# Last block of layer 2: order of the uncertainty branch, Tanh for Sigmoid, re-placed value products; one product of the up step ahead of the levels

## The chip, the cores and the metric

The kernel runs on one core of a Trainium2 chip. The metric is the time of one execution in microseconds on the device. A core has TensorE (PE), VectorE (DVE), ScalarE (ACT), GpSimd (POOL) and SyncE (SP, which issues DMAs). Each engine runs its own list of instructions in order; they wait for each other by semaphores. All matrix products are in fp32; each is two instructions on PE.

## The reference

A chain of four layers on 2048 tokens (64 sequences of 32) of width 512; each is a conditioning map and a feed-forward map, added to x. The change touches three places.

Layer 1's feed-forward is a gated product with a hidden width of 1376, its three weights quantised to 16 levels first:

```
h = silu(x @ w1.T) * (x @ w2.T);  x = x + h @ w3.T        (w1, w2, w3 after quantise and dequantise)
```

Layer 2's feed-forward (its input h is the output of layer 2's conditioning):

```
query = h @ Wq.T;  rq = query @ Wr.T;  rk = aux_keys @ Wr.T
scores = rq . rk / sqrt(48) + log_rel;  top 8 of 128 slots
w = softmax(query . key / 8 + log_rel) over the 8
aux_out = (w @ aux_values) @ Wvd.T @ Wvu.T
norm_var = log1p(var(h)) / (mean(log1p(var(h))) + 1e-6)
learned = gelu(h @ Wu1.T + bu1) @ Wu2.T + bu2
u = clip(norm_var * 0.5 + sigmoid(learned) * 2.5, 0, 5)
gate = sigmoid(gate_w1 * clip((u - 0.5) / 1.5, 0, 1) + gate_bias);  gate = 0 where gate < 0.05
result = h + gate * aux_out
```

Layer 3 averages x over each sequence under a mask, convolves the 32 (padded) means per feature, takes a sigmoid as a gate over x, and applies a linear map with a mixture of eight low-rank terms; the mixture weights of each second token come from a softmax, a top-2 threshold and a sigmoid.

## The kernel before

Tokens are handled in four blocks of 512 (TB = 4); x lies transposed in SBUF, features on partitions in four chunks (DC = 4). A product over one chunk and one block is 128x512; its two instructions take 0.43 us each. PSUM has eight banks of 128x512, `ps[:, bank, :]`.

*Up step of layer 1.* The 44 steps of the list `UPS` (L231) are pairs of token block and hidden chunk c (11 chunks, the last has 96 rows). `up(n)` on PE (L1040) computes both halves into banks n % 2 and 2 + n % 2. The steps with c = 10 put gate and up half into one bank (L1050 on). ACT (L804 to L825) runs, for each n, first its share of the *levels* (`parts_of(K_UP, n, ...)`, L747: a saturated comparison of a weight unit with one of 15 quantisation bounds), then the SiLU of step n, then a copy of a turned weight unit (`evac_quant`). DVE (L1608 to L1612) runs, for each n, its share of levels (L1513, L1516: add the step height; between units it prepares the next one, L1487 to L1494) and then, for c = 10 only, `hidden(n)` (up to L1605), the product of SiLU and up half; for the others POOL does it. PE's step n waits for the product or the copy of step n - 2, whose banks it overwrites. Step 33 is (block 3, c = 10).

*Layer 2, block tb.* On PE in this order: the conditioning's products, q (L1230 to L1234; two halves on 64 columns each), the wide uncertainty product into bank 4 (`p_gup`), 16 turns of Y to natural order for the variances (L1237), the scores (`p_sc`, banks 6 and 7), the learned product (bank 5, `p_lr`). In the last block, PE fills its waits with `slices`, narrow products for layer 3. ACT copies q, applies Gelu (L872), copies the learned column (L874), in the last block Ln of the variances (L878) and Sigmoid (L880), and then Exp of the selected scores (L885). DVE takes statistics (L1786), selects the top 8 per token (L1798 to L1803), and after the last block computes the uncertainty (L1805 to L1816), lets ACT take the gate (L888, Sigmoid), and scales the probabilities (L1824). PE turns them (L1266), ACT copies them (L893), `slices_aux` completes the narrow products, from which DVE computes the sequence gates (L1836 to L1848); `aux(n)` (16 products of the turned probabilities with the values) go to the banks `BANKS_AUX`, and DVE adds each to X (`add_aux`, L1830). `spread_gates` broadcasts the gates to banks 0 to 3, `base(n)` are layer 3's 16 products, `ranks` and `lift` its low-rank part.

ACT loads a function table (`ACT_TABLE_LOAD`) when the next function is not in the table it holds.

Of the kernel before, what the change touches and what calls it, by code (L numbers as in the profile page):

```python
# [16 lines left out]
P = 128  # L17
# [76 lines left out]
def build(nc, A, out):  # L94
    ctx = ExitStack()
    with ctx:
# [114 lines left out]
        gsc = sb("gsc", [P, 3])  # L211
# [22 lines left out]
        in_u = [Up[:, i % DC, i // DC * TW:(i // DC + 1) * TW] for i in range((TB - 1) * DC)]  # L234
        PLAIN = [i for i, (tb, c) in enumerate(UPS) if c < NH - 1]
# [129 lines left out]
        BANKS_AUX = 3 * [6, 7, 4, 5] + 2 * [4, 5]  # L365
# [351 lines left out]
        def _(act):  # L717
# [139 lines left out]
            for tb in range(TB):  # L857
# [12 lines left out]
                nc.scalar.activation(qT[0:BOT, TW // 2:], ps[BOT:, 1, 0:TW // 2], ACT.Copy).then_inc(s["a_q"], 1)  # L870
                act.wait_ge(s["p_gup"], tb + 1)
                nc.scalar.activation(gu, ps[:, 4, :], ACT.Gelu_apprx_tanh, bias=bu1[:, 0:1]).then_inc(s["a_gu"], 1)  # L872
                act.wait_ge(s["p_lr"], tb + 1)
                nc.scalar.activation(lrn[:, tb * NT:(tb + 1) * NT], ps[:, 5, 0:NT], ACT.Copy).then_inc(s["a_lr"], 1)  # L874
                if tb == TB - 1:

                    act.wait_ge(s["d_st"], TT + 1)
                    nc.scalar.activation(lv[:, :], var[:, :, 1], ACT.Ln, bias=1.0, accum_out=lvs[:, 0:1]).then_inc(s["a_lv"], 1)  # L878
                    act.wait_ge(s["a_lr"], TB)
                    nc.scalar.activation(gq[:, 0, :], lrn[:, :], ACT.Sigmoid, bias=gsc[:, 2:3]).then_inc(s["a_sg"], 1)  # L880
# [7 lines left out]
            nc.scalar.activation(gq[:, 2, :], gq[:, 1, :], ACT.Sigmoid, scale=gsc[:, 0:1], bias=gsc[:, 1:2]  # L888
# [30 lines left out]
        def _(pe):  # L919
# [250 lines left out]
            for tb in range(TB):  # L1170
# [54 lines left out]
                for c in range(DC):  # L1225
                    last = mm(ps[:, 4, :], l2u[:, c, :], Y[:, c, tok(tb)], c == 0, c == DC - 1)
                last.then_inc(s["p_gup"], 1)
# [16 lines left out]
                last.then_inc(s["p_sc"], 1)  # L1244
                pe.wait_ge(s["a_gu"], tb + 1)
# [23 lines left out]
            slices(1, range(0, 2))  # L1269
            pe.wait_ge(s["a_lv"], 1)  # L1270
            pe.wait_ge(s["a_lr"], TB)
            mm(ps[:, 5, 8:9], ones[:, :], lvs[:, 0:1], True, True).then_inc(s["p_lv"], 1)
            slices(1, range(2, DC))
            for tb in range(3):
                turn_probs(tb)
            slices_aux(0)
            turn_probs(3)
            slices_aux(1)

            def aux(n):  # L1280

                tb, oc = n // DC, n % DC
                if n >= 12:
                    pe.wait_ge(s["d_x3"], n - 1)
                elif n >= 4:
                    pe.wait_ge(s["d_x3"], n - 3)
                mm(ps[:, BANKS_AUX[n], :], v2[:, oc * P:(oc + 1) * P], PT[:, tok(tb)], True, True).then_inc(s["p_aux"], 1)

            def base(n):

                tb, oc = n // DC, n % DC
                if n < 2:
                    pe.wait_ge(s["a_g"], TB)
                    pe.wait_ge(s["d_x3"], DC)
                elif n < 4:
                    pe.wait_ge(s["d_x3"], 8 + BANKS_AUX.index(BANKS3[n]) + 1)
                elif n < 6:
                    pe.wait_ge(s["d_x3"], TB * DC - 5 + n)
# [7 lines left out]
            def spread_gates(pair):  # L1306
                pe.wait_ge(s["d_gex"], pair + 1)
                if pair == 0:
                    pe.wait_ge(s["a_zt"], TB)
                    pe.wait_ge(s["d_yd"], 2)  # L1310
                for j in range(2):
# [17 lines left out]
            for n in range(6):  # L1329
# [13 lines left out]
            base(2)  # L1343
            base(3)
# [5 lines left out]
            aux(12)  # L1350
            aux(13)
            for half in range(2):
                ranks(half)
            aux(14)
            aux(15)
# [10 lines left out]
        def _(dve):  # L1366
# [251 lines left out]
            ts(lbias[:, :, :], lbias[:, :, :], 5.0, None, ALU.mult, ALU.bypass)  # L1618
            for q in range(2):
# [187 lines left out]
            dve.wait_ge(s["p_lv"], 1)  # L1807
            dve.wait_ge(s["a_sg"], 1)
            ts(lvs[:, 1:2], ps[:, 5, 8:9], 1.0 / TOK, 1e-6, ALU.mult, ALU.add)
            link(V.reciprocal(lvs[:, 1:2], lvs[:, 1:2]))  # L1810
            ts(gq[:, 1, :], lv[:, :], lvs[:, 1:2], None, ALU.mult, ALU.bypass)
            ts(gq[:, 1, :], gq[:, 1, :], 0.5, None, ALU.mult, ALU.bypass)
            stt(gq[:, 1, :], gq[:, 0, :], 2.5, gq[:, 1, :], ALU.mult, ALU.add)
            ts(gq[:, 1, :], gq[:, 1, :], 0.0, 5.0, ALU.max, ALU.min)
            ts(gq[:, 1, :], gq[:, 1, :], 0.5, 1.0 / 1.5, ALU.subtract, ALU.mult)
            V.tensor_scalar(gq[:, 1, :], gq[:, 1, :], 0.0, 1.0, ALU.max, ALU.min).then_inc(s["d_un"], 1)  # L1816
# [128 lines left out]
```

## Time and profile before

| | us |
|---|---|
| median of three runs | 909.38 (909.37 to 910.17) |
| the profiled execution's own time | 909.91 |
| its span | 908.1 |
| PE busy | 856.7 (94%) |
| DVE busy | 615.3 (68%) |
| ACT busy | 411.9 (45%) |
| POOL busy | 153.2 (17%) |

The span runs from the first to the last recorded instruction; all positions are microseconds from its start. The weight loads of PE (PEld) overlap its products.

### The profile page before, as it was taken

Reading aid. Unit: us, or ns where it says so; the run is one execution under the profiler, and the core shown is the slowest. Engines: PE = TensorE matmul, PEld = TensorE weight load, DVE = VectorE, ACT = ScalarE, POOL = GpSimd, SP = SyncE. Lnnn points to the kernel's source line nnn. Section 1 sums busy time; section 2 is a strip of 40 time slices with the busy share of each in tenths; the row PEclk is TensorE's granted clock in tenths of the full one; section 3 lists DMA queues with packets and bytes.
Section 4 is the critical chain, followed back from the end, with each engine's and each line's share of the span. In section 5 each row is a group of like instructions: output and inputs, shape, how many; then the busy total and the mean of one; then the engine's idle time right before and its main releaser. Section 6 shows DMA issues by size and latency. Waiting matters only on the chain.

```text
span 908.1 us, 10585 instructions
## 1 busy us (share of the span) xinstructions
PE 856.7 (94%) x3265; PEld 458.4 (50%) x3266; DVE 615.3 (68%) x956; ACT 411.9 (45%) x531; POOL 153.2 (17%) x174
## 2 busy tenths in 40 slices
PE   0599999999999999999989999999999999979998
PEld 0496448998444444444444444444445555443442
DVE  7799987887888888899998744253452354256624
ACT  5124647886787777877878520000012132252100
POOL 5200008800121212221102110002401011010000
PEclk9999999999999999999999999999999999989999
DMA  6696138550000000100000110013010000002012
GB/s 184 239 340 229 58 116 282 199 209 31 23 23 24 5 13 32 33 17 16 32 1 0 41 49 1 0 58 128 15 51 1 1 0 1 1 1 46 35 58 93
DMA packets 34729, 60.98 MB, mean 67 GB/s; under 512 B 6040, under 2 KB 8424, under 8 KB 34040
## 3 DMA queue, kind: packets, MB, share of 16 engines
q1 hardware_dynamic: 33896, 60.26, 19.4%
q0 software_dynamic: 704, 0.10, 0.3%
q8 instruction: 26, 0.43, 0.2%
q14 instruction: 23, 0.19, 0.1%
q10 hardware_dynamic: 80, 0.01, 0.0%
HBM read 50.84 MB, written 8.47 MB: 65 GB/s over the span
## 4 chain that ended last, share of the span: by engine, by line
PE 86%; DVE 7%; issue 3%; POOL 2%; ACT 2%; DMA 0%; SPq 0%; POOLq 0%; ACTq 0%; DVEq 0%
PE ps L921 84%; DVE acc L1516 2%; DVE T L1516 1%; PE ps L979 1%; PE ps L1237 1%; DVE W2T L1377 1%; DMA T<-kpad 0%; PE ps L1266 0%; DVE raw L1494 0%; DVE amax L1487 0%; DVE Yp L1890 0%; POOL lan_i L648 0%; ACT Yp L862 0%; PE ps L1199 0%; DVE Yp L1529 0%
## 5 line engine op out<-in xcount | busy, mean ns | idle before, releaser
L747 ACT ACTIVATE above<-raw,cst 128x1024 bf16<-128x1024 f32 (+2 forms) x225 | 272.0, 1233 | 121.3 <-DVE acc L1516 43.7
L1516 DVE SCALAR_TENSOR_TENSOR acc<-above,acc 128x1024 f32<-128x1024 bf16 (+2 forms) x112 | 150.5, 1344 | 28.7 <-ACT above L747 24.7
L921 PE MATMUL ps<-Yp,W3T 128*128 (+1 forms) x740 | 159.5, 370 | 3.2 <-DVE Yp L1529 1.6
L921 PE MATMUL ps<-Up,W2T 128*128 128x512 f32 (+1 forms) x404 | 160.6, 593 | 0.0
L921 PE MATMUL ps<-Up,W1T 128*128 128x512 f32 x344 | 155.5, 594 | 2.8 <-DVE Up L1605 2.6
L1516 DVE SCALAR_TENSOR_TENSOR T<-above,T 128x1024 f32<-128x1024 bf16 (+1 forms) x84 | 118.1, 1405 | 22.7 <-ACT above L747 19.6
L921 PEld LDWEIGHTS ps<-Yp,W3T 128*128 128x128 f32 x740 | 102.3, 191 | 55.5 <-issue 52.9
L921 PEld LDWEIGHTS ps<-Up,W2T 128*128 128x128 f32 (+1 forms) x404 | 66.5, 177 | 85.9 <-issue 85.6
L921 PEld LDWEIGHTS ps<-Up,W1T 128*128 128x128 f32 x344 | 64.2, 190 | 82.1 <-issue 75.8
L921 PE MATMUL ps<-X,W3T 128*128 128x512 f32 (+1 forms) x176 | 77.8, 596 | 0.3 <-DVE X L1830 0.3
L921 PE MATMUL ps<-X,W2T 128*128 128x512 f32 x140 | 61.3, 594 | 0.0
L921 PEld LDWEIGHTS ps<-X,W3T 128*128 128x128 f32 (+1 forms) x176 | 32.9, 190 | 43.4 <-issue 41.8
L1636 DVE TENSOR_TENSOR Yp<-Yp,ps 128x512 f32<-128x512 f32 x14 | 9.4, 685 | 59.8 <-PE ps L921 59.8
L921 PE MATMUL ps<-Up,W3T 128*128 128x256 f32 (+3 forms) x196 | 45.5, 388 | 0.0
L921 PEld LDWEIGHTS ps<-X,W2T 128*128 128x128 f32 x140 | 26.3, 190 | 31.9 <-issue 31.9
L688 POOL TENSOR_TENSOR Yp<-Yp 128x512 f32<-128x512 f32 x13 | 19.9, 1534 | 120.3 <-ACT Yp L819 120.3
L921 PE MATMUL ps<-W1T,W2T 128*128 128x512 f32 (+1 forms) x144 | 36.0, 436 | 3.6 <-DVE W2T L1459 3.6
L708 POOL TENSOR_TENSOR X<-X,Yp 128x2048 f32<-128x2048 f32 x4 | 18.1, 4520 | 124.5 <-ACT Yp L862 124.5
L921 PEld LDWEIGHTS ps<-Up,W3T 128*128 128x128 f32 (+1 forms) x196 | 30.9, 191 | 13.4 <-issue 12.5
L688 POOL TENSOR_TENSOR X<-X,Yp 128x512 f32<-128x512 f32 x15 | 21.7, 1447 | 78.3 <-ACT X L819 78.3
L684 POOL COPY Yp<-X x44 | 34.1, 825 | 2.3 <-issue 2.3
L818 ACT ACTIVATE Yp<-ps 128x512 f32<-128x512 f32 x40 | 23.3, 582 | 20.4 <-PE ps L921 20.3
(336 smaller groups left out, 882.7 us busy)
## 6 DMA issues: line engine op xcount, KB each, us to landing
W3T<-in_wa SPq DMA_DIRECT2D x8, 1024.0 KB, 5.8
raw<-in_w SPq DMA_DIRECT2D x20, 256.0 KB, 3.0
W3T<-kpad SPq DMA_DIRECT2D x9, 512.0 KB, 6.9
Up<-in_xconv SPq DMA_DIRECT2D x4, 1024.0 KB, 12.1
X<-in_xT SPq DMA_DIRECT2D x4, 1024.0 KB, 8.7
W1T<-in_wa SPq DMA_DIRECT2D x4, 1024.0 KB, 6.5
xkeep<-X SPq DMA_DIRECT2D x4, 1024.0 KB, 4.7
X<-xkeep SPq DMA_DIRECT2D x4, 1024.0 KB, 9.0
```

The source lines that it names most:

```text
L684: pool.tensor_copy(Y[:, :, bass.ds(t * (4 * S) + i * S, S)], X[:, :, bass.ds(b * S, S)]).then_inc(s["g_xs"], 1)
L688: nc.gpsimd.tensor_tensor(slots[UPS[n]], slots[UPS[n]], sg[n % 2], ALU.mult).then_inc(s["g_h"], 1)
L708: nc.gpsimd.tensor_tensor(X[:, :, tok(tb)], X[:, :, tok(tb)], Y[:, :, tok(tb)], ALU.add).then_inc(s["g_xc"], 1)
L747: nc.scalar.activation(above[0:h, m % 2, 0:w], raw[0:h, u % 2, 0:w], ACT.Relu, scale=STEEP, bias=cst[0:h, C_BND + i:C_BND + i + 1]).then_i ...
L818: nc.scalar.activation(sg[n % 2][0:h, :], ps[0:h, n % 2, :], ACT.Silu).then_inc(s["a_silu"], 1)
L921: return nc.tensor.matmul(o, l, r, start=start, stop=stop, **kw)
L979: last = nc.tensor.transpose(dst, src, ident[0:h, 0:h])
L1237: last = nc.tensor.transpose(ps[:, BANKS_ST[t], c * P:(c + 1) * P], Y[:, c, tile(tb, t)], ident)
L1377: link(V.tensor_tensor(o, a, b, op))
L1516: V.scalar_tensor_tensor(out=ac, in0=src, scalar=float(STEPS[i]), in1=ac, op0=ALU.min, op1=ALU.add).then_inc(s["m_used"], 1)
L1636: V.tensor_tensor(o, a, b, op).then_inc(s["d_mix"], 1)
```

## The change

- On ACT, the SiLU of step 33 stands ahead of that step's levels; on DVE the product of step 33 does.
- In the last block of layer 2, PE's wide product (now `rise`) stands behind the scores; the mean product of the logarithms (now in bank 2) and one chunk of `slices(1)` follow it, then the learned product, then the other three chunks.
- On ACT, Ln stands ahead of Gelu. The learned column is not copied in the last block: sigmoid is computed as (1 + tanh(x/2)) / 2, the first twelve columns from the copies, the last four from PSUM. The gate, too, is a Tanh. Four small DVE instructions prepare the halved scales once.
- DVE computes the uncertainty with one clip to [0.5, 2.0] in place of two; the divisor 2 goes into the softmax's denominators.
- The value products use banks 2 and 3 too; aux(0) stands between the last turn and the second `slices_aux`, aux(6) and (7) between the spreads, aux(12) and (13) ahead of base(3), and aux(14) and (15) ahead of `ranks`. Additions 14 and 15 stand ahead of those of zq. The waits for banks follow the list.

```diff
-        BANKS_AUX = 3 * [6, 7, 4, 5] + 2 * [4, 5]
+        BANKS_AUX = [6, 7, 4, 5, 2, 3, 6, 7, 4, 5, 6, 7, 4, 5, 4, 5]
+        AUX_LAST = {b: n + 1 for n, b in enumerate(BANKS_AUX)}
...
             for n, (tb, c) in enumerate(UPS):
                 h = HCH[c]
-                for k in parts_of(K_UP, n, AD_LAST):
-                    level(k)
+                if n != LAST_REST:
+                    for k in parts_of(K_UP, n, AD_LAST):
+                        level(k)
                 act.wait_ge(s["p_gu"], n + 1)
...
+                if n == LAST_REST:
+                    for k in parts_of(K_UP, n, AD_LAST):
+                        level(k)
                 for u in turns_up(n):
                     evac_quant(u)
...
+                if tb == TB - 1:
+                    act.wait_ge(s["d_st"], TT + 1)
+                    nc.scalar.activation(lv[:, :], var[:, :, 1], ACT.Ln, bias=1.0, accum_out=lvs[:, 0:1]).then_inc(s["a_lv"], 1)
                 act.wait_ge(s["p_gup"], tb + 1)
                 nc.scalar.activation(gu, ps[:, 4, :], ACT.Gelu_apprx_tanh, bias=bu1[:, 0:1]).then_inc(s["a_gu"], 1)
...
+                else:
+                    act.wait_ge(s["a_lr"], TB - 1)
+                    nc.scalar.activation(gq[:, 0, 0:TT - NT], lrn[:, 0:TT - NT], ACT.Tanh, scale=0.5, bias=gsc[:, 3:4])
+                    act.wait_ge(s["p_lr"], TB)
+                    nc.scalar.activation(gq[:, 0, TT - NT:], ps[:, 5, 0:NT], ACT.Tanh, scale=0.5, bias=gsc[:, 3:4]
+                                         ).then_inc(s["a_sg"], 1)
...
-            nc.scalar.activation(gq[:, 2, :], gq[:, 1, :], ACT.Sigmoid, scale=gsc[:, 0:1], bias=gsc[:, 1:2]
+            nc.scalar.activation(gq[:, 2, :], gq[:, 1, :], ACT.Tanh, scale=gsc[:, 4:5], bias=gsc[:, 5:6]
...
+                if tb == TB - 1:
+                    rise()
+                    pe.wait_ge(s["a_lv"], 1)
+                    mm(ps[:, 2, 0:1], ones[:, :], lvs[:, 0:1], True, True).then_inc(s["p_lv"], 1)
+                    slices(1, range(0, 1))
...
+            for tb in range(3):
+                turn_probs(tb)
+            slices_aux(0)
+            turn_probs(3)
+            aux(0)
+            slices_aux(1)
+            for n in range(1, 6):
                 aux(n)
             spread_gates(0)
+            aux(6)
+            aux(7)
             spread_gates(1)
-            for n in range(6, 12):
+            for n in range(8, 12):
                 aux(n)
...
             for n in range(TB * NH):
+                if n == LAST_REST:
+                    hidden(n)
                 for k in parts_of(K_UP, n, AD_LAST):
                     level(k)
-                if n not in PLAIN:
+                if n not in PLAIN and n != LAST_REST:
                     hidden(n)
...
+            ts(lvs[:, 1:2], ps[:, 2, 0:1], 2.0 / TOK, 2e-6, ALU.mult, ALU.add)
+            link(V.reciprocal(lvs[:, 1:2], lvs[:, 1:2]))
+            ts(gq[:, 1, :], lv[:, :], lvs[:, 1:2], 1.25, ALU.mult, ALU.add)
             dve.wait_ge(s["a_sg"], 1)
...
+            stt(gq[:, 1, :], gq[:, 0, :], 1.25, gq[:, 1, :], ALU.mult, ALU.add)
+            V.tensor_scalar(gq[:, 1, :], gq[:, 1, :], 0.5, 2.0, ALU.max, ALU.min).then_inc(s["d_un"], 1)
             dve.wait_ge(s["a_pr"], TT)
-            link(V.reciprocal(gq[:, 3, :], den[:, :]))
+            ts(gq[:, 3, :], den[:, :], 2.0, None, ALU.mult, ALU.bypass)
+            link(V.reciprocal(gq[:, 3, :], gq[:, 3, :]))
             dve.wait_ge(s["a_gt"], 1)
...
+            stt(gq[:, 3, :], gq[:, 2, :], 1.0, gq[:, 3, :], ALU.add, ALU.mult)
+            stt(gq[:, 4, :], gq[:, 2, :], 2 * 0.05 - 1.0, gq[:, 3, :], ALU.is_ge, ALU.mult)
```

## Rows read from the trace of the kernel before

**Rows 1.** The page's first part: busy us, share of the span, instructions of each engine
```profile
PE 856.7 (94%) x3265; PEld 458.4 (50%) x3266; DVE 615.3 (68%) x956; ACT 411.9 (45%) x531; POOL 153.2 (17%) x174
```

**Rows 2.** Waits of PE, 200 to 909: who waited for whom, us, times, longest
```profile
PE ps L1266 <- DVE W1T L1824: 5.6, 1, 5.6
PE ps L921 <- DVE Up L1605: 2.6, 1, 2.6
```

**Rows 3.** Timeline 446 to 476: start us, us, engine, instruction, [idle before <- releaser]
```profile
456.12 1.36 PE L979 MATMUL ps<-cst,acc 128*128 128x128 f32 x11
461.46 4.94 DVE L1516 SCALAR_TENSOR_TENSOR T<-above,T 128x1408 f32<-128x1408 bf16 x3
463.18 1.47 ACT L747 ACTIVATE above<-raw,cst 128x1408 bf16<-128x1408 f32 x1 [5.62 <-DVE T L1516]
464.68 0.59 ACT L823 ACTIVATE Yp<-ps 64x512 f32<-64x512 f32 x1
...
466.44 0.69 DVE L1605 TENSOR_TENSOR Up<-Yp,ps 64x512 f32<-64x512 f32 x1
...
467.18 3.70 PE L921 MATMUL ps<-Up,W1T 128*128 128x512 f32 x8 [2.64 <-DVE Up L1605]
...
469.92 0.61 ACT L819 ACTIVATE Up<-ps 128x512 f32<-128x512 f32 x1
```

**Rows 4.** Timeline, the end of the up step
```profile
515.75 1.63 DVE L1522 TENSOR_TENSOR acc<-acc,amax 128x1408 f32<-128x1408 f32 x1
...
523.42 1.36 PE L979 MATMUL ps<-cst,acc 128*128 128x128 f32 x11
```

**Rows 5.** Windows: length, busy of PE PEld DVE ACT POOL, PE clock, DMA share, GB/s
```profile
466.00:467.00 1.00, 0.00 (x0) 0.00 (x0) 0.96 (x2) 1.00 (x4) 0.00 (x0) 1.00 0.00 0
...
668.00:669.00 1.00, 0.72 (x16) 0.55 (x20) 0.54 (x7) 0.73 (x2) 0.00 (x0) 0.50 1.00 389
...
811.00:811.50 0.50, 0.00 (x0) 0.00 (x0) 0.00 (x0) 0.50 (x1) 0.00 (x0) 0.72 0.00 0
...
818.00:818.50 0.50, 0.50 (x8) 0.05 (x1) 0.00 (x0) 0.00 (x0) 0.00 (x0) 0.95 0.00 0
```

**Rows 6.** Timeline 780 to 806: q with the wide product, Gelu, the learned product
```profile
794.30 5.58 PE L921 MATMUL ps<-Yp,raw 128*64 128x256 f32 x24
...
799.91 0.69 ACT L872 ACTIVATE Up<-ps,bu 128x512 f32<-128x512 f32 x1 [1.55 <-PE ps L921]
...
803.33 0.95 PE L921 MATMUL ps<-wu,Up 128*128 128x1 f32 x8
```

**Rows 7.** Timeline 805 to 815: row maximum, gate, first scaling, first turns
```profile
807.92 0.69 DVE L1803 TENSOR_REDUCE Up<-Up 128x4 f32<-128x512 f32 x1
...
812.86 0.18 DVE L1383 SCALAR_TENSOR_TENSOR gq<-gq 128x16 f32<-128x16 f32 x1 [1.88 <-ACT gq L888]
...
813.28 2.50 DVE L1824 TENSOR_TENSOR W1T<-W1T,gq 128x512 f32<-128x512 f32 x4
...
814.03 2.98 PE L1266 MATMUL ps<-cst,W1T 128*128 128x128 f32 x12 [5.62 <-DVE W1T L1824]
```

**Rows 8.** Chain of waits in order of time: start us, us, engine, tile, line
```profile
809.05 1.65 ACT W1T L885 x8
810.71 1.28 ACT L888
```

**Rows 9.** Timeline 819 to 857: slices, row sums, the layer 3 gate's Sigmoid, additions
```profile
819.80 1.07 PE L921 MATMUL ps<-W1T 128*32 128x512 f32 x8 [0.69 <-ACT W1T L893]
...
821.00 0.69 DVE L1836 TENSOR_TENSOR Yp<-ps,W2T 128x512 f32<-128x512 f32 x1 [0.57 <-PE ps L921]
...
824.63 0.26 ACT L906 ACTIVATE W3T<-W3T 128x64 f32<-128x64 f32 x1 [1.63 <-DVE W3T L1843]
...
825.25 1.98 PE L921 MATMUL ps<-W1T,above 128*128 128x512 f32 x4 [0.76 <-DVE X L1830]
...
856.23 4.13 PE L921 MATMUL ps<-X,W3T 128*128 128x512 f32 x9 [0.26 <-DVE X L1830]
```

More of the change, by code:

```diff
@@ L210, in build @@
         wu2 = sb("wu2", [P, 1])
-        gsc = sb("gsc", [P, 3])
+        gsc = sb("gsc", [P, 6])
         lan_i = sb("lan_i", [P, TT], i32)
@@ L878, in _ @@
                     nc.scalar.activation(lv[:, :], var[:, :, 1], ACT.Ln, bias=1.0, accum_out=lvs[:, 0:1]).then_inc(s["a_lv"], 1)
-                    act.wait_ge(s["a_lr"], TB)
-                    nc.scalar.activation(gq[:, 0, :], lrn[:, :], ACT.Sigmoid, bias=gsc[:, 2:3]).then_inc(s["a_sg"], 1)
+                act.wait_ge(s["p_gup"], tb + 1)
+                nc.scalar.activation(gu, ps[:, 4, :], ACT.Gelu_apprx_tanh, bias=bu1[:, 0:1]).then_inc(s["a_gu"], 1)
+                if tb < TB - 1:
+                    act.wait_ge(s["p_lr"], tb + 1)
+                    nc.scalar.activation(lrn[:, tb * NT:(tb + 1) * NT], ps[:, 5, 0:NT], ACT.Copy).then_inc(s["a_lr"], 1)
+                else:
[4 more added lines that the diff above has]
+                                         ).then_inc(s["a_sg"], 1)
                 act.wait_ge(s["d_am"], tb + 1)
@@ L1224, in _, with rise @@
                 last.then_inc(s["p_q"], 1)
-                for c in range(DC):
-                    last = mm(ps[:, 4, :], l2u[:, c, :], Y[:, c, tok(tb)], c == 0, c == DC - 1)
-                last.then_inc(s["p_gup"], 1)
+                def rise():
+                    for c in range(DC):
+                        last = mm(ps[:, 4, :], l2u[:, c, :], Y[:, c, tok(tb)], c == 0, c == DC - 1)
+                    last.then_inc(s["p_gup"], 1)
+                if tb + 1 < TB:
+                    rise()
                 for t in range(NT):
@@ L1267, in turn_probs @@
                 last.then_inc(s["p_pt"], 1)
[L1269 to L1278, printed above, removed]
+            slices(1, range(1, DC))
             def aux(n):
                 tb, oc = n // DC, n % DC
[L1283 to L1286, printed above, removed]
+                before = [k for k in range(n) if BANKS_AUX[k] == BANKS_AUX[n]]
+                if before:
+                    pe.wait_ge(s["d_x3"], before[-1] + 1)
                 mm(ps[:, BANKS_AUX[n], :], v2[:, oc * P:(oc + 1) * P], PT[:, tok(tb)], True, True).then_inc(s["p_aux"], 1)
@@ L1343, in _ @@
             base(2)
+            aux(12)
+            aux(13)
             base(3)
@@ L1349, in _ @@
             last.then_inc(s["p_wt"], 1)
-            aux(12)
-            aux(13)
+            aux(14)
+            aux(15)
             for half in range(2):
                 ranks(half)
-            aux(14)
-            aux(15)
             pe.wait_ge(s["l_bm"], 16 * DC)
@@ L1618, in _ @@
             ts(lbias[:, :, :], lbias[:, :, :], 5.0, None, ALU.mult, ALU.bypass)
+            ts(gsc[:, 3:4], gsc[:, 2:3], 0.5, None, ALU.mult, ALU.bypass)
+            ts(gsc[:, 4:5], gsc[:, 0:1], 0.5 / 1.5, None, ALU.mult, ALU.bypass)
+            stt(gsc[:, 5:6], gsc[:, 0:1], -0.5 / 1.5, gsc[:, 1:2], ALU.mult, ALU.add)
+            ts(gsc[:, 5:6], gsc[:, 5:6], 0.5, None, ALU.mult, ALU.bypass)
             for q in range(2):
@@ L1883, in _ @@
             V.tensor_tensor(tm3, tm3, ss3[:, 4, :].unsqueeze(2).to_broadcast([P, 8, E]), ALU.mult).then_inc(s["d_w3"], 1)
-            add_aux(range(12, 14))
+            add_aux(range(12, 16))
             dve.wait_ge(s["l_zq"], 16 * DC)
```

26 lines of the change are left out of this document (6 added, 20 removed).

## The prediction

> **What bounds the kernel now.** I read the busy line of the page first [rows 1]: TensorE (PE) is busy for 856.7 of the 908.1 us span, so only its idle time, or work put ahead of it, can be won. The list of waits names that idle time from 200 us on [rows 2]: one wait of 5.6 us at L1266 for VectorE (DVE), one of 2.6 us at L921 for DVE's L1605, the others 1.0 us and less. The change touches both places. Between them PE runs on without a listed wait, so what it wins at the first place reaches the second, and from there the end, unless another engine then comes too late. I follow the timeline at both places.
>
> First place, the up step of layer 1 [rows 3]. PE ended the remainder step of the last token block (n = 33) and turned a unit at 456.12. It then ran step 34 (6.9 us) and stopped at 467.18 - 2.64 = 464.54, since step 35 wants the product of step 33. DVE made that at 466.44: it waited for ScalarE's (ACT's) SiLU at 464.68 and came out of its own three levels (4.94 us from 461.46). The SiLU stood behind three level instructions, of which the third waited 5.62 us for DVE and began at 463.18. The input of the SiLU had been there since about 456.1.
>
> Second place, the last block of layer 2. PE finished the slices at 808.4 (814.03 less 5.62) and stood until 814.03, when DVE had scaled the first probabilities [rows 7]. The chain of waits [rows 8] shows why: table loads of 1.28 us lie between Gelu, Ln, Sigmoid, Exp and Sigmoid again; Exp runs 809.05 to 810.70, the next load to 811.99, the gate's Sigmoid (0.4) to 812.4.
>
> **Part 1, SiLU and product ahead of the levels.** Nothing is added, the same instructions change places [rows 3]. SiLU at 456.3 (the 0.2 us that ACT needs after PE's end), done at 456.9. DVE is done with the product of step 32 at 457.4, makes that of step 33 in 0.7, by 458.1, far ahead of 464.54. So the 2.64 us go. What is late next? ACT's two first levels move behind the SiLU, to 456.9 to 459.7; DVE wants them only when it has prepared the next unit, and that moves back by the 0.7 us of the product: its first level starts at 462.2 in place of 461.46, ACT's third level at 463.9 in place of 463.18. But the SiLU no longer stands between that level and the following eviction, so the eviction starts at 465.4 against 465.29: the level stream is 0.1 us late. ACT's copy for step 34 ended at 469.92 + 0.59 = 470.51 [rows 3], now 470.6; PE wants it for step 36 at 464.54 + 6.9 = 471.45. The slack is 0.8 us there and over 2 us at every later step. At the end of the stage DVE's last scaling, begun at 515.75, is done at 517.38, and PE asks for it at 523.42 [rows 4]; 2.6 us earlier it still waits for nothing. Value 2.6 us; bounds 1.8 (the slack eaten by a slip of twice 0.8) and 2.64.
>
> **Part 2, the last block up to the first turn of the probabilities.** q plus the wide product (rise) take 5.58 us in 24 instructions from 794.30, of which the 8 of 128x512 at 0.43 are 3.43 [rows 6]. Rise moves behind the scores, so the turns to natural order, the statistics and the scores come 3.43 us earlier: DVE's row maximum is there at 804.49 + 0.69 = 805.2 for 807.92 + 0.69 = 808.61 [rows 7]. DVE had waited for PE at the head of this chain and follows it. Everything here is moved on PE, nothing added: scores end at 799.9, rise at 803.33, the mean product 803.6, one chunk of slices (8 instructions, 0.96) 804.6, the learned product (0.88 [rows 6]) 805.5, three chunks of slices 808.4, as before.
> ACT: Ln's load goes ahead at 797.1, Ln itself at 800.5 when the variances are in, Gelu's load to 802.1, Gelu at 803.33 + 0.31 = 803.64 to 804.33 (0.69, [rows 6]). PE has not yet asked for it, at 804.6. The first Tanh follows at once, the second at 805.6, done at 805.85. The trace has no Tanh. Between Gelu and Exp a load of 1.28 stands in every block; either it comes in front of the Tanh and is over by 805.6, or it comes behind the last Tanh, or both. I take behind, since before the load stands directly in front of Exp and not in front of the copy that follows Gelu: 805.87 to 807.15. Four Exp of 1.65 us together [rows 8]: 808.8. The gate's Tanh (0.4) ends at 809.2, with no load in front if Exp and Tanh lie in one table. DVE's eight small instructions on the uncertainty become five, of about 0.2 us each, and are over by 806.3, beside ACT's load: worth nothing. The doubled denominators and their reciprocal (0.45) run beside the gate's Tanh, to 809.3. Before, DVE started 0.45 us after ACT's end (812.4 to 812.86 [rows 7]) and no view says why; I let it stand, from 809.2 to 809.65. Two instructions 0.4, the first scaling 0.70, and 0.05: PE turns at 810.9. That is 814.03 - 810.9 = 3.1 us; bounds 1.4 (a load on both sides of the Tanh, 0.4 later, and one more at the gate, 1.28) and 4.5 (one load, in front, 0.9, and no 0.45).
> The Trainium skill ("ScalarE: Activation LUTs", sections What ACT_TABLE_LOAD costs and Table sets) puts a switch at about 2.66 us, since 1.38 us of drain come on top, and lists tanh beside exp in one set. Here the loads take 1.28 and the next activation starts 0.02 us behind; the trace contradicts the drain. With it, part 2 would give 3 x 1.38 = 4.1 us more, as three of the four loads behind 804.3 leave the path.
> The four instructions that prepare gsc's new columns (0.2 each) stand behind DVE's last scaling [rows 4], where it has nothing but small preparations until PE has ended the up step: nothing. The Sigmoid of the sequence gate (L906) now needs its own load; it goes ahead while ACT waits 1.63 us for the convolution [rows 9]: nothing, and 0.3 us at most.
>
> **Part 3, from the first turn to the first base product.** Let T be the start of the first turn. Before it is 814.03 and base(0) starts at 834.34: 20.3 us, of which PE needs 16 turns of 0.12, 16 slice instructions 1.9, 24 aux instructions of 0.43 (10.3), gate spreads 1.8, together 15.9. The granted clock was 0.5 of full, 1.2 GHz, from 811.2 (2.8 us of idle had passed) to 818.0, and full in the 2.64 us gap of the up step [rows 5]. Now PE idles from 808.4 to 810.9, 2.5 us. I take full clock. Then: turn 0 at T to 0.47, turn 1 at 0.6, ACT's copies 0.60 each from T + 0.65, so turn 2 at 1.3, the first slice products at 1.95 to 2.9, turn 3 to 3.4, aux(0) to 4.25 in the hole in which before PE waited for ACT's fourth copy (0.69 us up to 819.80 [rows 9]), the second slice products to 5.2. In the old order these ended at T + 6.8 (820.80) without aux(0).
> aux(1) to aux(5) now run without a wait to 9.5, for aux(4) and (5) have free banks 2 and 3; before aux(4) waited for the first addition until 825.25 [rows 9]. DVE bounds next: from the second slice products it took 821.00 to 824.60 for the row sums and the convolution [rows 9]; two additions (1.2) and the first gate (0.7) follow: 5.2 + 0.2 + 3.6 + 1.2 + 0.7 = T + 10.9. PE idles 1.4. Spread 0 to 11.8, aux(6), (7) to 13.5, spread 1 must wait until DVE has added aux(5) (four additions of 0.62 behind the gates at 11.5): 14.0 to 14.9, aux(8) to (11) to 18.4. base(0) at T + 18.4 against 20.3: 1.9 us. Bounds: 0.4 if the clock falls again (PE worked 4.0 us at 1.2 GHz before, 2.0 lost at most, a quarter of it in holes: 1.5), 2.9 if the DVE chain overlaps better by 1 us.
>
> **Part 4, to the last additions.** From base(0) PE has 20 us of base products, the same in number; the order of aux(12) to (15), ranks and base(3) changes. Additions 14 and 15 are done before base(4), which waited for them at 856.23, 21.9 us after base(0) [rows 9]; now lift(0) waits about 0.5 us for the first zq product, and base(4) comes 21.6 after base(0). Value 0.3, bounds -0.4 (the lifts wait a whole 1.1 us more) and 0.7.
>
> **Sum.** 2.6 + 3.1 + 1.9 + 0.3 = 7.9 us. The profiled execution took 909.91 (span 908.1 and 1.8 around it); less 7.9 it is 902.0. The median of the runs lies 0.5 lower, at 909.38, so I predict 901.5.
>
> **Rivals.**
> A. The load comes in front of the first Tanh and none in front of Exp. Exp then starts at 806.3 for 807.15 and T is 0.9 earlier: 900.6. For: the one load between Gelu and Exp serves both if Tanh lies with Exp but not with Gelu. Against: the row only shows that a load exists. By the list of the Trainium skill ("ScalarE: Activation LUTs", Table sets: tanh in the exp set, the approximated gelu apart) it would go this way; no run here shows it yet.
> B. The clock falls again, for PE's idle is followed by 3 us of short turns with holes. For: it was at 0.5 at 668 [rows 5] after a gap of only 0.7 us behind narrow products, and here after 2.8. Against: it held over 2.64 [rows 5]. That takes up to 1.5 us: 903.0.
> C. The waits move: the re-placement of aux only shifts PE's idle to the spreads, because DVE's chain from the second slice products is unchanged, and part 4 gives nothing: 901.5 + 2.2 = 903.7. For: DVE is busy nearly throughout. Against: the earlier second slice products start that very chain 1.6 us sooner.
> D. Slower: the clock falls and is not given back within the stretch. Its 15.9 us of PE work take 31.8 at 1.2 GHz, 15.9 more: 901.5 + 15.9 = 917.4. It decides from 15.8 us at 1.2 GHz on, of which half is lost. Against: it came back after 4.0 us of work at 818.0.
> E. The moved SiLU makes the level stream so late that PE waits at step 36 or at the last turned unit, and part 1 gives nothing: 904.1. For: ACT now waits with an empty queue behind the SiLU. Against: 0.8 us of slack, counted above.
>
> **How the numbers follow.** Chances: forecast 0.44, A 0.20, B 0.17, C 0.09, E 0.06, D 0.04. Within 0.2% of before (1.8 us, about what a measurement tells from no change) is 907.6 to 911.2; only a sum of B, C and E lands there. D holds most of the slower side. Faster 0.94, same 0.03, slower 0.03. The range takes in A with the upper bounds (2.64, 4.5, 2.9, 0.7 would be 10.7: 898.7; I stop at 899.3) and B and C with some of E: 904.5.
>
> **What would show it.** Step 1: no PE wait at L1605, PE continuous over 464. Step 2: scores on DVE 3.4 us earlier against the stage's start, two loads fewer, PE's gap ahead of L1266 2.5 us. Step 3: granted clock 1.0 through the turns, base(0) 18.4 us after them, waits of 1.4 and 0.5 us at the spreads. Wrong it would be above all through a third load around the Tanh, a fallen clock, or a new wait in steps 34 to 43.

## The result and the profile after

The changed kernel took 906.03 us (median of 7 executions, 903.18 to 906.73) against 910.17 us (909.37 to 911.15) of the kernel before on the same chip: ratio 0.9948, 95% interval 0.9934 to 0.9962. The direction was right, the size was not: 901.5 us was forecast and the range ended at 904.5. Measured twice more beside other kernels, it gave 905.36 (0.9956 [0.994, 0.9971]) and 905.25 us (0.9943 [0.9929, 0.9957]). Every median here is of the fast executions; two slow ones, of 1536.06 us (e12) and 1153.44 us (e13), are left out.

The profiled execution took 904.57 us with a span of 902.7, 5.4 less than before; it is 1.5 us quicker than the median, and the medians differ by 4.1. The busy line of its page, where PE's busy time has not fallen [rows 1]:

```profile
PE 857.8 (95%) x3265; PEld 458.5 (51%) x3266; DVE 616.6 (68%) x958; ACT 410.2 (45%) x530; POOL 156.3 (17%) x174
```

The waits of PE from 200 to 909 us, against [rows 2]. The 2.6 us of the up step are gone, 5.6 have become 2.2, and two waits are new (1.1 at the gate spreads, 0.9 at the lifts); the wait of 0.7 near 664 was there before (it is at L1630 in that kernel):

```profile
PE ps L1286 <- DVE W1T L1846: 2.2, 1, 2.2
PE ps L931 <- DVE W3T L1870: 1.1, 1, 1.1
PE ps L931 <- DVE Yp L1912: 0.9, 1, 0.9
PE ps L931 <- DVE X L1654: 0.7, 1, 0.7
```

The timeline of the up step, against [rows 3]. The SiLU of step 33 (L826) starts 0.20 us behind the turned unit, the products follow at once, and step 35 starts without a wait. ACT's third level (462.85) and the copy for step 34 (468.84) are where the working put them:

```profile
455.18 1.36 PE L989 MATMUL ps<-cst,acc 128*128 128x128 f32 x11
...
455.38 0.59 ACT L826 ACTIVATE Yp<-ps 64x512 f32<-64x512 f32 x1 [1.61 <-PE ps L931]
455.73 1.30 DVE L1623 TENSOR_TENSOR Up<-Yp,ps 64x512 f32<-64x512 f32 x2
...
462.85 1.47 ACT L749 ACTIVATE above<-raw,cst 128x1408 bf16<-128x1408 f32 x1 [4.02 <-DVE T L1534]
...
463.44 3.60 PE L931 MATMUL ps<-Up,W1T 128*128 128x512 f32 x8
...
468.84 0.61 ACT L822 ACTIVATE Up<-ps 128x512 f32<-128x512 f32 x1
```

The timeline of the last block of layer 2, from q to the first turns, against [rows 6, 7]. One table load is left between Gelu and the turns, in front of Exp; the first turn stands 16.19 us behind q's start (790.49), where it stood 19.73 behind it (794.30 to 814.03) before:

```profile
790.49 1.73 PE L931 MATMUL ps<-Yp,raw 128*64 128x256 f32 x14
...
799.67 0.69 ACT L881 ACTIVATE Up<-ps,bu 128x512 f32<-128x512 f32 x1 [1.42 <-PE ps L931]
...
800.26 0.29 ACT L887 ACTIVATE gq<-lrn,gsc 128x12 f32<-128x12 f32 x1
...
801.77 0.26 ACT L889 ACTIVATE gq<-ps,gsc 128x4 f32<-128x4 f32 x1 [1.22 <-PE ps L931]
802.05 1.28 ACT L895 ACT_TABLE_LOAD   x1
...
804.90 0.38 ACT L898 ACTIVATE gq<-gq,gsc 128x16 f32<-128x16 f32 x1
...
805.94 2.50 DVE L1846 TENSOR_TENSOR W1T<-W1T,gq 128x512 f32<-128x512 f32 x4
...
806.68 2.52 PE L1286 MATMUL ps<-cst,W1T 128*128 128x128 f32 x12 [2.24 <-DVE W1T L1846]
```

The windows of the same trace (length, busy of PE, PEld, DVE, ACT, POOL, granted clock, DMA share, GB/s) show what the waits don't: PE is busy, at half its clock, in the turns and again at the lifts. Before, it was at half in the turns and full at the lifts, as these two windows of the kernel before show:

```profile
815.00:816.00 1.00, 1.00 (x6) 0.70 (x5) 0.78 (x2) 0.60 (x1) 0.00 (x0) 0.50 0.00 0
...
855.00:856.00 1.00, 0.98 (x8) 0.15 (x8) 1.00 (x2) 0.00 (x0) 0.00 (x0) 1.00 0.00 0
```

The changed kernel:

```profile
808.00:809.00 1.00, 1.00 (x6) 0.71 (x4) 0.43 (x1) 0.60 (x1) 0.00 (x0) 0.50 0.00 0
809.00:810.00 1.00, 1.00 (x7) 0.20 (x8) 0.00 (x0) 0.60 (x1) 0.00 (x0) 0.50 0.00 0
...
849.00:850.00 1.00, 1.00 (x5) 0.23 (x2) 0.91 (x3) 0.00 (x0) 0.00 (x0) 0.50 0.06 16
850.00:851.00 1.00, 1.00 (x2) 0.48 (x3) 0.96 (x2) 0.00 (x0) 0.00 (x0) 0.50 0.00 0
```

The lifts in the timeline, PE against DVE, with the new wait of 0.94 us and eight narrow products that take 1.79 us:

```profile
847.21 2.48 DVE L1912 SCALAR_TENSOR_TENSOR Yp<-ps,Yp 128x512 f32<-128x512 f32 x4 [0.44 <-PE ps L931]
...
848.05 1.79 PE L931 MATMUL ps<-Yp,raw 32*128 32x512 f32 x8 [0.94 <-DVE Yp L1912]
...
849.77 15.00 PE L931 MATMUL ps<-X,W3T 128*128 128x512 f32 x32
```

The span can be cut at five starts that every trace has: the turned unit of step 33, step 35, q of the last block, the first turn T, and base(0). Worked out from the starts in the two timelines:

```
                          before   after   gain   forecast
start of span to unit     456.12   455.18   0.94    0
unit to step 35            11.06     8.26   2.80    2.6   (part 1)
step 35 to q              327.12   327.05   0.07    0
q to T                     19.73    16.19   3.54    3.1   (part 2)
T to base(0)               20.31    20.06   0.25    1.9   (part 3)
base(0) to the end         73.76    75.96  -2.20    0.3   (part 4)
```

Parts 1 and 2 gave what was forecast. Of part 3 next to nothing arrived, and behind base(0) 2.2 us went lost, so 5.4 us are left of 7.9. The first row is no gain of the change: the start of that unit lies anywhere from 454.33 to 458.17 in the 17 traces of this case. Without it the trace shows 4.5 us, near the 4.1 of the medians.

### The profile page after: what moved, and what is told of

Read it like the earlier page. It is cut to its first block, busy times and chain, and to the rows that moved or that the text cites. A ratio compares the mean times of both kernels' runs of the same rounds, so it can differ in the third digit from the quotient of the medians.

```text
span 902.7 us, 10586 instructions
## 1 busy us (share of the span) xinstructions
PE 857.8 (95%) x3265; PEld 458.5 (51%) x3266; DVE 616.6 (68%) x958; ACT 410.2 (45%) x530; POOL 156.3 (17%) x174
## 4 chain that ended last, share of the span: by engine, by line
PE 91%; DVE 3%; issue 2%; POOL 2%; ACT 1%; DMA 0%; SPq 0%; POOLq 0%; ACTq 0%; DVEq 0%
PE ps L931 89%; PE ps L989 1%; PE ps L1252 1%; DVE acc L1534 1%; DVE W2T L1395 1%; DMA T<-kpad 0%; PE ps L1286 0%; POOL lan_i L650 0%; ACT Yp L868 0%; DVE Yp L1547 0%; PE ps L1209 0%; ACT W1T L895 0%; SPq L534 0%; POOL gsc L645 0%; POOL kk L645 0%
```

## The experiments

Two theories stood at the start. The clock theory: each stretch in which the clock is at half is a cost of its own, and it ate part 3 and most of what part 4 lost. The rival: the waits only moved, and the re-placement of the auxiliary products costs PE idle time at any clock. All kernels below were timed in five rounds beside the kernel before; those of one group shared a chip.

**First group: the parts alone, and the gap filled.** The kernel before had 909.49 us.

The SiLU and its product alone (e1):

```
-                for k in parts_of(K_UP, n, AD_LAST):
-                    level(k)
+                if n != LAST_REST:
+                    for k in parts_of(K_UP, n, AD_LAST):
+                        level(k)
...
+                if n == LAST_REST:
+                    for k in parts_of(K_UP, n, AD_LAST):
+                        level(k)
...
+                if n == LAST_REST:
+                    hidden(n)
```

> The kernel before with part 1 alone (SiLU and product of step 33 ahead of the levels). Theory: part 1 is whole in the changed kernel (step 35 starts 2.8 us earlier against the turned unit ahead of it) and nothing of the shortfall lies there: 2.6 to 2.8 us faster than before, no wait for the product of step 33, all later rows as before. Rival E (the level stream comes late and eats it): 0 to 1 us faster, with a new wait of PE in steps 36 to 43.

Measured 906.01 us, 0.9962 [0.9948, 0.9976]: 3.5 us by the medians, where 2.6 to 2.8 were expected, which lies inside the interval. Unit to step 35 is 8.26 us as in the changed kernel. The spans of the two traces differ by 4.4; what goes beyond 2.8 is the scatter of the start (455.49 for 456.12) and a stretch at half clock near 668 us that this trace lacks, less 0.5 us that it loses behind the first turn.

The branch alone (e2: q, scores, rise; Ln early; Tanh; one clip; the old auxiliary order):

```
+                if tb == TB - 1:
+                    rise()
+                    pe.wait_ge(s["a_lv"], 1)
+                    mm(ps[:, 2, 0:1], ones[:, :], lvs[:, 0:1], True, True).then_inc(s["p_lv"], 1)
```

> The kernel before with part 2 alone (scores ahead of the wide product, Tanh, one clip; value products in their old banks and order). Theory that the granted clock took the rest: the first turn of the probabilities comes 3.5 us earlier than in before, and the total gains 3.5 us, or up to 2 us less where the clock falls in another part of the stretch behind it; base(0) 19 to 20.3 us behind the first turn, and from there to the end as in before (73.8 us). Rival that moved work is paid back later by waits for VectorE: gain under 2 us with the clock at full.

Measured 905.37 us, 0.9955 [0.9941, 0.9969]: 4.1 us, with the expected 3.5 inside the interval. q to T is 16.19 us, T to base(0) 20.44, base(0) to the end 73.82. Its timeline (of the slowest of the five executions, 909.0 us) has step 35 behind the same gap as before, yet with eight products in 5.40 us, where they took 3.70 before [rows 3]:

```profile
469.23 5.40 PE L925 MATMUL ps<-Up,W1T 128*128 128x512 f32 x8 [2.64 <-DVE Up L1615]
```

So the length of this gap doesn't decide: the clock held over it in the trace of before, and fell behind it here and in e3.

The re-placement alone (e3: banks 2 and 3, the new order, the new tail):

```
-        BANKS_AUX = 3 * [6, 7, 4, 5] + 2 * [4, 5]
+        BANKS_AUX = [6, 7, 4, 5, 2, 3, 6, 7, 4, 5, 6, 7, 4, 5, 4, 5]
...
```

> The kernel before with parts 3 and 4 alone (value products re-placed). My prediction had it at 2.2 us faster. Theory now: by itself it gives 0 to 1 us, since with the clock at 1.2 GHz through the turns VectorE's chain starts no earlier than about 1 us, and the ranks, which now stand directly ahead of the lifts, leave a wait of 0.9 us and a second fall of the clock that costs up to 1.7 us; from base(0) to base(4) 22 to 23 us against 21.9. Rival (the re-placement is good and only part 2's gap spoils it): 1.5 us or more faster, from base(0) to base(4) 21.6.

Measured 911.33 us, 1.0021 [1.0012, 1.003]: by itself this part makes the kernel slower, by 1.8 us, which neither side of the expectation had (0 to 1 us faster, or 1.5 and more). T to base(0) is 20.36 us (20.31 before), base(0) to the end 75.94 (73.76 before). So both the missing gain of part 3 and the loss of part 4 are there without parts 1 and 2. (Its clock fell behind the gap of the up step, too; in the trace of before it fell near 668 instead.)

The changed kernel with two products whose result nobody uses, in PE's gap ahead of the turns (e4):

```
             slices(1, range(1, DC))
+            pe.wait_ge(s["d_un"], 1)
+            for k in range(2):
+                mm(ps[:, 2, :], ident, X[:, k, tok(TB - 1)], True, True)
```

> The changed kernel with two needless 128x512 products (four instructions, 1.7 us) in PE's gap of 2.2 us ahead of the turns; their result is not used. Clock theory: the granted clock stays at full through the turns, the first turn starts at the same place, base(0) follows after 18.4 to 18.9 us in place of 20.1, so 1.2 to 1.7 us faster than the changed kernel (about 5.5 us faster than before). Rival (the waits for VectorE set this stretch, whatever the clock): base(0) stays 20 us behind the first turn and the total is that of the changed kernel, 4.1 us faster than before, or slower by what the products push.

Measured 901.51 us, 0.9916 [0.9901, 0.993]: 8.0 us under the kernel before, where about 5.5 were expected. The changed kernel, in other groups, was 4.1 to 4.7 us under it, so more work made the kernel 3.3 to 3.8 us faster (3.0 by the spans, 899.7 against 902.7). Its timeline has the turns as early as in the changed kernel, and base(0) 18.77 us behind them:

```profile
804.38 1.98 PE L931 MATMUL ps<-X,cst 128*128 128x512 f32 x4
806.70 1.26 PE L1286 MATMUL ps<-cst,W1T 128*128 128x128 f32 x8 [0.33 <-DVE W1T L1849]
...
825.47 3.60 PE L931 MATMUL ps<-X,W3T 128*128 128x512 f32 x8
...
846.78 1.14 PE L931 MATMUL ps<-Yp,raw 32*128 32x512 f32 x8 [0.95 <-DVE Yp L1915]
```

Its windows are at full clock in the turns, and at the lifts too:

```profile
808.00:809.00 1.00, 0.87 (x8) 0.58 (x12) 0.44 (x1) 0.79 (x2) 0.00 (x0) 1.00 0.00 0
809.00:810.00 1.00, 1.00 (x11) 0.31 (x4) 0.11 (x1) 0.40 (x1) 0.00 (x0) 1.00 0.00 0
...
849.00:850.00 1.00, 1.00 (x3) 0.38 (x3) 0.96 (x3) 0.00 (x0) 0.00 (x0) 1.00 0.00 0
```

The second was not expected: base(0) to the end is 74.23 us, 0.5 over the old tail in place of 2.2. The filling stands 40 us ahead of the lifts, and the lifts wait 0.95 us as before; why the clock held there is open.

**Second group, beside the changed kernel again** (905.36 us, the kernel before 909.64; its trace: T to base(0) 20.34, base(0) to the end 75.93).

> The changed kernel again, as the control of this group. 4 us faster than before if its earlier median (906.03) holds; both theories expect the granted clock at 0.5 through the turns or at the lifts in most executions.

A one-column Exp behind the last Gelu, its result unused (e5):

```
+                if tb == TB - 1:
+                    nc.scalar.activation(gq[:, 5, 0:1], gsc[:, 2:3], ACT.Exp)
```

> The changed kernel with a one-column Exp on ScalarE directly behind the last Gelu (its result is not used), so that the table with Exp is loaded there and serves the Tanh behind it. Theory: rival A of the prediction can be had by order: no load between the last Tanh and Exp, Exp starts 0.9 us earlier, the gap of PE ahead of the turns is 1.3 us in place of 2.2 us, and with so short a gap the clock more often stays at full: 0.9 to 2.5 us faster than the control. Rival (the Tanh is not in Exp's table or the load lies on the path anyway): one load more and no gain, 0 to 1.3 us slower than the control.

Measured 902.1 us, 0.9908 [0.9891, 0.9924]: 3.3 us under the control, above the 2.5 expected at most. ACT's timeline shows the load behind Gelu, and both Tanh and the Exp without another (nor is there one ahead of the gate's Tanh, at 804.90):

```profile
801.62 1.28 ACT L883 ACT_TABLE_LOAD   x1
802.91 0.20 ACT L883 ACTIVATE gq<-gsc 128x1 f32<-128x1 f32 x1
803.02 0.29 ACT L889 ACTIVATE gq<-lrn,gsc 128x12 f32<-128x12 f32 x1
803.22 0.24 ACT L891 ACTIVATE gq<-ps,gsc 128x4 f32<-128x4 f32 x1
803.36 0.39 ACT L897 ACTIVATE W1T<-Up 128x128 f32<-128x128 f32 x1
```

This is rival A, made by hand: PE's gap is 1.02 us in place of 2.24. q to T is 14.97 us for 16.20. Behind it the clock stays full, and T to base(0) is 18.76 us: the same as with the filling, without any added product. At the lifts the clock falls as in the control (75.94), though they start where they start in e4, behind the same wait:

```profile
806.70 1.26 PE L1288 MATMUL ps<-cst,W1T 128*128 128x128 f32 x8 [1.02 <-DVE W1T L1848]
...
825.46 3.60 PE L933 MATMUL ps<-X,W3T 128*128 128x512 f32 x8
...
846.77 1.94 PE L933 MATMUL ps<-Yp,raw 32*128 32x512 f32 x8 [0.95 <-DVE Yp L1914]
```

base(4) ahead of the four lifts (e6):

```
-            last_base = 3
+            base(4)
+            last_base = 4
```

> The changed kernel with base(4) ahead of the first four lifts, where PE waits 0.9 us for VectorE's first zq product behind the narrow ranks. Clock theory for the tail: no wait and no fall of the clock at the lifts, the end 0.9 to 2.6 us earlier against base(0), total 1 to 2.5 us faster than the control. Rival (the end is set by VectorE's results, which now come 3.4 us later for the first four): 0 to 1 us.

Measured 901.83 us, 0.9911 [0.9891, 0.993]: 3.5 us under the control, above the 1 to 2.5 expected. base(0) to the end is 73.43 us, 2.5 under the control's and 0.3 under the old tail: the lifts run in 1.14 us without a wait, the clock is full there. The edit takes away the wait and the narrow neighbour at once, so it doesn't tell which of the two the clock needs.

```profile
846.87 3.70 PE L931 MATMUL ps<-X,W3T 128*128 128x512 f32 x8
850.50 1.14 PE L931 MATMUL ps<-Yp,raw 32*128 32x512 f32 x8
```

Part 4 alone taken back (e7): aux(12) to (15), ranks and additions in the old order.

```
             base(2)
-            aux(12)
-            aux(13)
             base(3)
...
+            aux(12)
+            aux(13)
+            for half in range(2):
+                ranks(half)
             aux(14)
             aux(15)
-            for half in range(2):
-                ranks(half)
...
```

> The changed kernel with the old order from base(1) on (aux(12), aux(13), ranks, aux(14), aux(15), lifts; additions 14 and 15 behind zq). Theory that part 4 is a loss, not the gain of 0.3 us that I forecast: from base(0) to base(4) 21.9 us again, no wait of 0.9 us and no fall of the clock at the lifts, total 0.5 to 2 us faster than the control. Rival (part 4 is neutral and only the clock's luck differs): within 0.3 us of the control.

Measured 903.0 us, 0.9929 [0.9914, 0.9944]: 2.4 us under the control, just above the expected 0.5 to 2; base(0) to the end 73.74.

**Third group: combinations** (the kernel before 910.04 us). Filling and base(4) first together (e8):

> The changed kernel with both edits that helped singly: two unused 128x512 products (K = 128) in TensorE's gap ahead of the turns, and base(4) issued ahead of the four lifts. Theory (each stretch at half clock is paid for by itself): alone the filling gave 3.9 us over the changed kernel of the same call and base(4) first 3.5; both take away time at half clock around 808 and around 848 us, and the filling's own traces had none at 848 either, so the sum is no 7.4 but the two dips of some 1.3 us each, the lifts' wait of 0.9 and the gap's rest: 0.989 to 0.991 of the kernel before, 899.5 to 901 us, with the granted clock full from 670 us on. Rival (the two overlap wholly, and what is left is the scatter of the start and of the up step): 0.9914, the same as the filling alone, 901.5 us.

Measured 900.98 us, 0.9904 [0.989, 0.9917]: as expected by the theory in the median (0.9904), though the interval reaches the rival's 0.9914. T to base(0) 18.76 us, to the end 73.47, and from 640 us on no stretch at half clock in which PE works.

One filling product, base(4) first and the early Exp (e9):

> The changed kernel with one unused 128x512 product in the gap ahead of the turns, base(4) ahead of the lifts, and a one-column Exp directly behind the last Gelu, so that the table load of 1.28 us lies beside TensorE's products and Tanh and Exp follow without one. Theory: the gap ahead of the turns ends 1.2 us earlier than in the changed kernel (2.24 to about 1.0 us, as the Exp alone showed), half filled by the product; the turns run at full clock, and the lifts don't wait: the first turn at about 805.5 us where the start is equal, 0.988 to 0.990, 898.5 to 900.5 us. Rival: the first turn waits for the filling product and the gain over the run with filling and base(4) first is nothing.

Measured 899.6 us, 0.9885 [0.987, 0.99]: as expected. q of the last block to T is 15.0 us by its timeline (790.76 to 805.73), against 16.2.

Part 4 taken back, again. The label of this run speaks of a filling; the kernel has none and is that of e7:

> The changed kernel with the last products of the auxiliary head in their old order, run again beside the two others as the kernel that takes back part 4 alone. Theory (part 4 costs 0.5 us at full clock and some 1.1 more where the clock falls at the lifts): 0.992 to 0.994, 902.5 to 904 us, between the changed kernel (0.9948 and 0.9956 so far) and the two others. Rival (the order of the tail does nothing and the last call's difference was scatter): 0.995 to 0.9955, as the changed kernel.

Measured 901.0 us, 0.9906 [0.9891, 0.9921], 2 us less than the same kernel in the second group and 1.5 below the 902.5 to 904 expected. The stretches agree (20.34 and 73.80 us, there 20.21 and 73.74); this trace has no half clock near 665, the other had. The executions say the same: three of the four here had a mean granted clock of 0.998 (900.49 to 901.22 us) and one 0.996 (902.58), all five there 0.996 (902.5 to 903.95). The kernel is the same, so the 2 us are scatter, and the scatter goes with the clock.

**Fourth group: what part 3 is worth at full clock** (the kernel before 909.98 us). Parts 1 and 2 alone (e12):

> The kernel before with parts 1 and 2 alone: the SiLU ahead of the levels and the shorter branch, the auxiliary products and their banks as before. Theory (parts 3 and 4 give 0.25 at half clock and take 2.2 behind base(0)): about 2 us faster than the changed kernel of the same call, 902 to 904 us, 0.992 to 0.994; base(0) to the end 73.8 us against 75.9, the first turn to base(0) 20.3 to 20.5. Rival (parts 3 and 4 help by what my sum gave, and parts 1 and 2 give less together than singly): as the changed kernel or slower, 905.5 to 907, 0.996.

Measured 903.32 us, 0.9913 [0.9893, 0.9933], in the expected 902 to 904; the changed kernel beside it 905.25:

> The changed kernel again, beside the three others of this call: 0.995 to 0.9956 of the kernel before as in its two measurements so far, 905 to 906 us, base(0) to the end 75.9 us with the clock at half at 848.

So parts 3 and 4 together cost 1.9 us by the medians (the intervals touch), 1.74 by the stretches behind T (20.45 + 73.81 against 20.05 + 75.95). Then the same with the gap filled by two unused products (e13):

> The kernel of parts 1 and 2 alone with two unused 128x512 products in the gap ahead of the turns. It shows the old order of the first twelve auxiliary products at full clock. Theory A (my 1.9 us for part 3 was the clock's loss booked to the order): first turn to base(0) 18.7 to 19.2 us, as with part 3 and the filling (18.77), and the whole time some 1.5 us under the unfilled one, 900.5 to 902. Theory B (the banks' waits were real, at full clock too): 20.0 to 20.3 us at full clock, the whole time 1 us or less under the unfilled one.

Measured 899.8 us, 0.9896 [0.988, 0.9912], 3.5 us under the unfilled one where some 1.5 were expected, with the clock full through the turns. Near 665 its clock is full as well and the unfilled one's was not, so the totals say less here than the stretch does. Its timeline has 18.87 us from T to base(0), in the old order of the auxiliary products:

```profile
804.21 1.26 PE L1285 MATMUL ps<-cst,W1T 128*128 128x128 f32 x8 [0.33 <-DVE W1T L1846]
...
823.08 3.60 PE L930 MATMUL ps<-X,W3T 128*128 128x512 f32 x8
```

Theory A holds (18.7 to 19.2 us expected, by theory B 20.0 to 20.3): at full clock the new order needs 18.77, the old one 18.87.

Last, parts 1 and 2 with the early Exp and one filling product, both unused (e14):

> Parts 1 and 2 alone, with a one-column Exp directly behind the last Gelu and one unused 128x512 product in the gap ahead of the turns. By theory A the first turn comes 1 us earlier than in the changed kernel, the stretch to base(0) takes 18.8 and the rest 73.8: 899.5 to 901 us, 0.9885 to 0.990, within 0.4 us of the kernel that has parts 3 and 4 too with base(4) ahead of the lifts (899.6 us, 0.9885). By theory B it is 1.3 us slower than that: 901 to 902.

Measured 899.57 us, 0.9885 [0.9869, 0.9901]: 10.4 us under the kernel before and the fastest with e9 (899.6), without parts 3 and 4. Both beat the changed kernel by some 5.7 us (905.25 beside e14; 905.36 in another group than e9).

The stretches of all traces, us, by what the kernel has there:

```
T to base(0)         half clock in the turns         full clock
  old order      20.31 (before) 20.83 20.44 20.45    18.87 18.87
  new order      20.06 (after) 20.34 20.05 20.36     18.77 18.76
                 20.10 20.21 20.34                   18.76 18.75
base(0) to end
  old tail       none                                73.74 to 73.82, 8 traces, before among them
  new tail       75.93 to 75.96, 5 traces            74.23 (e4)
  base(4) first  none                                73.42 73.43 73.47
```

## Why the prediction was off, step by step

**Part 1** (forecast 2.6, at most 2.64) was right, and 0.16 above its bound: 2.80. Step 34's last row ends at 460.01 + 3.60 = 463.61, and step 35 starts at 463.44: the rows of PE overlap by 0.17, which a wait measured from a row's end leaves out. SiLU 0.2 us behind the unit, the third level at +7.67 (forecast +7.8), the copy done at +14.3 (+14.5), no new wait in the later steps. Rival E did not come.

**Part 2** (3.1) was right, 0.4 short. Counted from q's start, the load in front of Exp stands at +11.56 (forecast +11.57), Exp ends at +14.5 (+14.5), T is at +16.19 (+16.6). DVE followed ACT's end (805.28) by 0.24 us in place of the 0.45 that I had let stand, 0.04 behind the end of its own reciprocal (805.23 + 0.25 = 805.48); the gate's Tanh started 0.1 inside Exp; and the working's last steps (809.65 + 0.4 + 0.70 + 0.05) give 810.8, not 810.9. Together that is the 0.4. No load stands in front of the first Tanh, so the approximated Gelu's table serves Tanh as well; rival A did not come by itself, since the one load between Gelu and the turns stood in front of Exp (802.05) and not in front of Tanh. In e5, with an Exp ahead of the Tanh, it stood there (801.62). The Trainium skill ("ScalarE: Activation LUTs", section Table sets) lists tanh in the set of exp and names the approximated Gelu only as separate from gelu's set. That exp and tanh share a set, e5 agrees with (Exp's load, then Tanh at 803.02 without one); that the approximated Gelu has no Tanh beside it, as I had read the list, this case contradicts. The drain of 1.38 us, which I had set aside, is not there after the change either: the second Tanh ends at 802.03, the load runs from 802.05 to 803.33, and Exp starts at 803.34.

**Part 3** (1.9) failed at one sentence: "I take full clock". PE stood 2.24 us, near the forecast 2.5, and then the clock fell: rival B. The part gave 0.25. I held the 2.64 us gap of the up step [rows 5] against B; e2 and e3 have the same gap with the clock down behind it. The error lay deeper than that choice. Before, the turns had been at half clock too, so my 1.9 compared an old order at 1.2 GHz with a new one at 2.4 GHz, and booked the difference to the order. Measured with the clock alike: 0.1 us at full clock (18.87 against 18.77; my 18.4 for the new order was 0.4 short), the clock 1.3 to 1.6. My waits were right in kind (aux(4) no longer waits; 1.1 us at the first spread, forecast 1.4; at the second none, forecast about 0.5) and PE's idle only moved from one to the other: that half of rival C was true.

**Part 4** (+0.3, bounds -0.4 and 0.7) failed in its sign and left its bounds: -2.2. Two steps of it failed. The forecast 21.6 us from base(0) to base(4) is the old 21.9 less the 0.26 that base(4) waited; the 0.5 that the same sentence gives to the lifts' wait is not in it, so its own numbers made a small loss and not a gain. The lifts wait 0.94 us, and the part is -0.5 at full clock (74.23 in e4 against 73.76 before). The second step is a term put at nothing: no fall of the clock at the lifts. Their wait comes between narrow products (ranks 8x512 ahead, lifts 32x512 behind) and the clock falls there: 1.7 us more (75.94 in e5 against 74.23 in e4, the same order and the same wait), in five of the six traces that have this tail. The row at 668 [rows 5], a fall after 0.7 us behind narrow products, stood in the prediction as an argument for rival B at the turns; it wasn't held against the lifts. With base(4) between ranks and lifts, in three traces, the clock stayed full.

**Sum.** 7.9 + 0.20 + 0.44 - 1.65 - 2.50 + 1.01 (start and the steps between, which part of no edit is) = 5.40 us. Rival B alone (903.0) had the mechanism and not its second place. The four terms at their own lower bounds (1.8, 1.4, 0.4, -0.4) would have given 906.2, so the range, which stopped at 904.5, was narrower than the bounds that it stood on; that 906.03 lies just inside them is luck, since parts 1 and 2 came whole and part 4 fell below its bound.

What is not settled: why e4's clock held at the lifts, and what decides it near 665 us, where it is at half in 9 of 17 traces of all kinds of kernels; at half, 32 narrow and 8 wide products take 5.96 us (664.44 to 670.40 in the changed kernel's trace), at full 4.53 (664.32 to 668.85 in that of its second measurement):

```profile
664.44 1.90 PE L931 MATMUL ps<-X,l2r 128*8 128x128 f32 x32 [0.74 <-DVE X L1654]
666.27 4.29 PE L931 MATMUL ps<-X,raw 128*128 128x512 f32 x8
670.40 0.27 PE L1164 MATMUL ps<-cst,Up 128*128 128x128 f32 x1
```

```profile
664.32 1.06 PE L931 MATMUL ps<-X,l2r 128*8 128x128 f32 x32 [0.74 <-DVE X L1654]
665.31 3.70 PE L931 MATMUL ps<-X,raw 128*128 128x512 f32 x8
668.85 0.27 PE L1164 MATMUL ps<-cst,Up 128*128 128x128 f32 x1
```

Much of the scatter between executions of one kernel is of this size or twice it, and it goes with the clock. In e13 the three executions with a mean granted clock of 0.999 took 898.63 to 899.8 us, the two with 0.996 and 0.997 took 901.37 and 902.21; in e14 897.91 and 898.09 at 0.999, 899.57 to 900.87 at 0.997; in e12 900.16 and 900.94 at 0.998, 903.32 to 904.74 at 0.996. Where in the span those executions lost the clock is not shown, since only one of each kernel has a trace.

## What to carry to other kernels

Before a stretch of the old trace is compared with a worked out one, bring both to the same granted clock: a gain that is "20.3 before, 18.4 by my count" may be nothing but the clock. Where PE idles next to narrow or short products, price the fall of the clock as its own term, once per such place, and look whether the change makes a new one: here a new wait of 0.9 us cost 2.2, 1.7 of it by the clock. The remedies are cheap: a wide product placed in the gap (one whose result is needed, as base(4), or even an unused one), or the table load moved out of it.

## What the runs showed of the hardware that was not expected

- The length of a wait of PE did not decide whether the clock fell behind it, with PE 94 to 95% busy over the span. It fell in all eight traces with 2.24 us ahead of the turns, in five of six with 0.94 at the lifts, in two of three with 2.64 in the up step (e2 and e3, not before) and in 9 of 17 with 0.74 near 665 to 672. It stayed full behind 1.02 us ahead of the turns (e5) and behind 1.09 at the first spread, in all 11 traces of the new order. Each fall cost 1.3 to 2.0 us.
- Two unused 128x512 products (1.98 us of PE time) in a gap of 2.24 us made the kernel 3.3 to 3.8 us faster by the medians, each against the kernel before in its own group; 1.3 to 1.6 of it is in the turns behind them, 1.7 at the lifts.
- Tanh ran directly behind the approximated Gelu without a table load (799.67 + 0.69, Tanh at 800.26), and behind Exp's load as well (e5, 803.02).
